# Local attention on one core: masks of head groups side by side, small masking products behind them

## What is computed

```python
Q, K, V = heads(x @ wq), heads(x @ wk), heads(x @ wv)        # 16 heads of 16
i, j = arange(64)[:, None], arange(128)[None, :]
base = (j > i) & (j <= i + 64)                               # window of 64 keys
blk0 = (block > 0) | (j >= 64)                               # block 0 has no block before it
sc = where(base & blk0, einsum(Qb, [K_prev, K_own]) / 4, -inf)
local = softmax(sc) @ [V_prev, V_own]
rem = softmax(where(n <= s // 16, GQ @ pooled(GK).T / 4, -inf)) @ pooled(GV) @ r_out_w
out = (sigmoid(Q . gl) * local + sigmoid(Q . gr) * rem) @ w_out
```

## Time and profile before

| | us |
|---|---|
| median of 3 runs | 2291.6 |
| lowest and highest | 2290.39, 2296.07 |
| the profiled execution | 2287.45 |
| its span, first to last instruction | 2285.7 |
| TensorE busy with products | 2010.9 (88%) |
| VectorE busy | 1642.6 (72%) |
| ScalarE busy | 1221.4 (53%) |

### The profile page before, as it was taken

One profiled execution on the slowest core, in us unless ns is written; L12 is line 12 of the kernel. 1 busy time (PEld: TensorE's weight loads), 2 busy tenths in 40 slices (PEclk: granted clock), 3 DMA queues, 4 the chain that ended last, 5 costly groups with the idle time before them and its releaser, 6 DMA issues. The chain is left out here.

```text
span 2285.7 us, 74481 instructions
## 1 busy us (share of the span) xinstructions
PE 2010.9 (88%) x32248; PEld 1276.1 (56%) x32248; DVE 1642.6 (72%) x2668; ACT 1221.4 (53%) x1870; POOL 495.5 (22%) x804
## 2 busy tenths in 40 slices
PE   3996999999987985798878999999999999999985
PEld 2663565656655654457854555555555555555543
DVE  6776555554546778776676888888888888888847
ACT  3772232313234765223315777777776777777754
POOL 0003000000000000000014544345443544435410
PEclk8998898999999996899967999999999999999997
DMA  3001000000000000342485544545544555455312
GB/s 113 1 1 28 21 2 20 3 20 3 1 21 1 1 1 5 103 144 97 190 294 139 144 128 129 133 127 140 132 128 127 145 142 133 115 138 138 101 29 74
DMA packets 273791, 195.11 MB, mean 85 GB/s; under 512 B 206744, under 2 KB 260310, under 8 KB 273210
## 3 DMA queue, kind: packets, MB, share of 16 engines
q1 hardware_dynamic: 262586, 139.27, 23.9%
q0 software_dynamic: 10496, 50.75, 5.9%
q10 hardware_dynamic: 384, 0.33, 0.0%
HBM read 91.69 MB, written 93.88 MB: 81 GB/s over the span
## 5 line engine op out<-in xcount | busy, mean ns | idle before, releaser
L2158 DVE TENSOR_REDUCE a1c_nm<-a1c_S 128x1 f32<-128x1024 f32 x512 | 609.6, 1218 | 83.6 <-PE a1c_S L2245 83.1
L2092 ACT ACTIVATE a1c_PT<-a1c_ST 128x1024 f32<-128x1024 f32 x499 | 509.8, 1022 | 67.0 <-PE a1c_ST L2245 64.3
L2109 ACT ACTIVATE a1c_Pb<-a1c_S,a1c_nm 128x192 f32<-128x192 f32 (+1 forms) x512 | 212.2, 415 | 202.5 <-DVE a1c_nm L2158 201.2
L2031 POOL TENSOR_TENSOR a1c_lt<-a1c_lt 128x256 f32<-128x256 f32 (+5 forms) x448 | 254.0, 567 | 35.5
L2148 DVE COPY a1c_PbT<-a1c_T 96x512 f32<-96x512 f32 x256 | 175.8, 687 | 98.5 <-PE a1c_T L2277 96.1
L2245 PE MATMUL a1c_ST<-a1c_Q,a1c_KR 57*128 57x256 f16 (+2 forms) x1066 | 176.5, 286 | 29.6 <-ACT a1c_PT L2092 19.3
L2245 PE MATMUL a1c_S<-a1c_KL,a1c_Q 54*32 54x512 f16 (+11 forms) x3136 | 193.7, 327 | 0.3
L2245 PE MATMUL a1c_S<-a1c_KR,a1c_Q 54*32 54x512 f16 (+13 forms) x2816 | 182.0, 317 | 12.8 <-DMA a1c_Gx<-a_bias 10.2
L2245 PE MATMUL a1c_S<-a1c_Gx,ident 64*32 64x96 f32 (+2 forms) x4352 | 186.1, 242 | 0.0
L2023 POOL DMA_DIRECT2D a_band<-a1c_Pb x128 | 71.0, 555 | 494.7 <-ACT a1c_Pb L2109 494.6
L2277 PE MATMUL a1c_T<-ident,a1c_Pb 128*96 128x128 f32 x1024 | 169.5, 289 | 0.8 <-DVE a1c_mhl L2172 0.8
(11 more groups left out here) (366 smaller groups left out, 4096.4 us busy)
## 6 DMA issues: line engine op xcount, KB each, us to landing
a_band<-a1c_Pb POOLq DMA_DIRECT2D x128, 384.0 KB, 3.4
a_bias<-a1b_G SPq DMA_DIRECT2D x32, 768.0 KB, 9.3
a1c_Gx<-a_bias SPq DMA_DIRECT2D x128, 192.0 KB, 4.4
a1c_Dt<-a_band SPq DMA_DIRECT2D x128, 126.0 KB, 3.7
a1c_Q<-a_qk SPq DMA_DIRECT2D x192, 64.0 KB
a1c_Vw<-a_values SPq DMA_DIRECT2D x64, 102.0 KB, 3.0
a1c_KL<-a_qk SPq DMA_DIRECT2D x96, 64.0 KB
a1c_KR<-a_qk SPq DMA_DIRECT2D x90, 64.0 KB
```

The costliest lines, as they stand in the source:

```text
L2031: add = lambda o, x, y: nc.gpsimd.tensor_tensor(o, x, y, ALU.add)
L2092: nc.scalar.activation(PT[:, q % 8, :, :], place(q), ACT.Exp).then_inc(s["exp"], 1)
L2109: nc.scalar.activation(Pb[:, band_slot(I, c), w0:w1], SP[:, t % 2, I * P - 32 + w0:I * P - 32 + w1], ACT.Exp, bias=nm[:, t // 16 % 2, col: ...
L2158: nc.vector.tensor_reduce(nm[:, t // 16 % 2, col:col + 1], SP[:, t % 2, :], AX.X, ALU.max, negate=True).then_inc(s["max"], 1)
```

## The change

In `scores`, the four masks are issued with nothing between them but the two waits (c = 0 and 1, wait, c = 2 and 3), and the four small products follow behind the last mask. In `by_key`, the small products leave the loop over the masks and stand behind all four masks and behind the wait for `mTe`, ahead of the four products with `sel`. The numbers of instructions and their operands are the same. The jobs with g = 1 keep their order.

```diff
-                for c in range(4):
-                    if n == 0 and c % 2 == 0:
-                        pe.wait_ge(s["lmax"], 4 * b + 3 + c // 2)
-                    elif c % 2 == 0:
-                        pe.wait_ge(s["smax"], 2 * (b * NJ + n) - 1 + c // 2)
-                    mm(R[:, c, :], ones64[tri(c), 0:2, :].rearrange("p a x -> p (a x)"), band[tri(c), :, :].rearrange("p a x -> p (a x)"),
-                       start=True, stop=False, skip_group_check=True)
-                    if g == 0:
+                for a in range(2):
+                    if n == 0:
+                        pe.wait_ge(s["lmax"], 4 * b + 3 + a)
+                    else:
+                        pe.wait_ge(s["smax"], 2 * (b * NJ + n) - 1 + a)
+                    for c in (2 * a, 2 * a + 1):
+                        mm(R[:, c, :], ones64[tri(c), 0:2, :].rearrange("p a x -> p (a x)"),
+                           band[tri(c), :, :].rearrange("p a x -> p (a x)"), start=True, stop=False, skip_group_check=True)
+                if g == 0:
+                    for c in range(4):
                         mm(R[0:WIN, c, 0:WIN], ones64[tri(c), 0, :], wall[tri(c), :], start=False, stop=False, skip_group_check=True)
...
                     mm(R[:, c, :], band[tri(c), 0, :], ones64[tri(c), :, :].rearrange("p a x -> p (a x)"), start=True, stop=False,
                        skip_group_check=True)
-                    if job(n - 2)[0] == 0:
-                        mm(R[0:WIN, c, 0:WIN], wall[tri(c), :], ones64[tri(c), 0, :], start=False, stop=False, skip_group_check=True)
...
                     pe.wait_ge(s["mTe"], 2 * b + g + 1)
+                    if g == 0:
+                        for c in range(4):
+                            mm(R[0:WIN, c, 0:WIN], wall[tri(c), :], ones64[tri(c), 0, :], start=False, stop=False,
+                               skip_group_check=True)
```

## The result

The changed kernel takes 2255.97 us (median of 4 runs, 2253.49 to 2260.46) against 2293.75 for the kernel before beside it: a ratio of 0.984, 95% interval 0.982 to 0.986, 37.8 us by the medians and 36.9 by the ratio. A second series gave 2254.53 against 2287.94, ratio 0.985 (0.983 to 0.987), 33 us. The forecast was 2263.6 with a range from 2255 to 2281; the time lies 1 us inside the range's fast end, and the second series' median half a us outside it.

The account below looks back on a forecast made before the run. In the local stage, TensorE's small fixed-cost pieces compete with the trip to VectorE or ScalarE and back. Savings of 3.65 (scores) plus 3.34 (keys) a batch, 28.0 us in four, took 2291.6 to 2263.6 us; range 2255 to 2281.

Parts of the forecast that it names:

- Masks side by side: Changed score and key jobs: four uncovered masks cost 0.54 us, instead of 1.84 with the small products between.
- W: Cost of the four small products behind the masks: taken as 0.20 us, with ends 0.145 and 0.58.
- small products one by one: Rival: small products cost 0.145 us each even side by side; saving 15.8 us, time 2275.8; chance 0.18.
- The trip over VectorE: Score jobs: from one job's products through VectorE's reduction and back to the next job's products, 4.18 us against 4.90 before.
- Key jobs, 4.72: Key jobs 3 to 5: ScalarE's exponentials decide, giving 4.72 us from one masks' block end to the next.
- TensorE waits about 0.9 us in key job 4: Key job 4: TensorE came at 405.43 before and now waits about 0.9 us, as ScalarE sets the pace.
- The cover lost by the first two small products: Small products of c = 0 and 1 now stand behind the second semaphore wait, adding to the trip over the other engine.
- VectorE's remaining cover: Key jobs: VectorE idled 1.60 us before its second reciprocal; job 2 takes 1.10, leaving 0.5.
- The sum, 28.0 us: Local stage: score jobs save 3.65 and key jobs 3.34 us, 6.99 a batch, 28.0 over four batches.
- The same two dips of the clock in each batch: Expected sign: granted clock still falls to 1.2 GHz after the gates and between scores and keys in every batch.
- the dip behind the gates goes away: Rival: the denser block keeps 2.4 GHz after the gates, about 1 to 1.5 us a batch, 2258 us; chance 0.11.
- Waiting lowers the clock in the changed jobs (slower): Rival: TensorE's new waits in five of eight changed jobs bring 1.2 GHz; 12 us slower, 2303.6; chance 0.04.

Follow-up runs that it names:

- the one-half kernel: Changed kernel with all four small products reading operands from the first half of the partitions: 2262.67 us, ratio 0.9885 to the kernel before.
- the kernel by pairs: Changed kernel with two masks, their small products, the wait, then the other two masks and theirs: 2266.78 us, ratio 0.990 to the kernel before.
- the halves: Kernel before with only the score part of the change, 2269.13 us (ratio 0.991), or only the key part, 2275.21 us (ratio 0.994).

## Why the prediction was right

- **Masks side by side, 0.54 us for four.** 0.53 measured. The rows of the jobs with g = 1 were the right ones to price it with.
- **W = 0.20.** 0.18 measured, between the ends 0.145 and 0.58. Halfway between "the second pair is free" and "it costs as much" was near; the one-half kernel shows that even without pairing W would have been 0.24. The high end, and with it the rival of small products one by one (given a chance of 0.18), is refuted: the price was the switch of shapes. So is its variant in which the second pair waits for the first (W up to 0.29): even four products from one half start 0.24 / 4 = 0.06 us apart on average.
- **The trip over VectorE, 4.18 us.** 4.16 measured. **Job 2, ended by TensorE itself, 4.24 us:** 4.21, where it was 5.35. **Key jobs, 4.72:** 4.70.
- **TensorE waits about 0.9 us in key job 4.** The idle time there is 0.52 us: the 0.9 is the distance from the first masks to the third, 393.44 - 392.52 = 0.92, and holds the first two masks too.
- **The cover lost by the first two small products.** Counted whole in W; the kernel by pairs shows the cover was worth 0.03 to 0.04 us a job.
- **VectorE's remaining cover, 0.5 us.** 0.47 measured.
- **The sum, 28.0 us.** 28.4 at full clock, in two profiles of each kernel, and 15.0 and 13.7 in the halves.
- **"The same two dips of the clock in each batch."** This step failed. The rival that the dip behind the gates goes away came true in part, in one or two of four batches, and in these B could be free of it too. The profiles put 3.1 and 6.2 us of the gain down to the clock. That is the part of the gap between forecast and time that the runs show. I had given it a chance of 0.11 as a case apart, all or nothing; it should have been a term of its own in the sum, since the block right behind the gates was among those that the change makes denser.
- **Waiting lowers the clock in the changed jobs (slower).** Refuted: key jobs 3 to 5 keep 4.70 us with up to 0.52 us of waiting (job 4), in all 8 batches of the two profiles.
- **The range.** Its low end adds up to 2258 - 1.8 - 2 = 2254.2 and was written as 2255. The mechanism of the sum was right; that the time stayed inside the written range was partly luck, since nothing in the sum held the clock's part, and the second series' 2254.53 lies between the two figures.

The medians differ by 33 and 38 us; order and clock explain 31 to 35 of it in the profiles. The stages outside the local one took 1783.4 and 1780.9 us in the two profiles before and 1782.7 and 1786.0 in those after, and 1781 to 1791 over all thirteen profiles. So the remainder is inside what differs from run to run. The clock's part, 3 to 6 us, is smaller than that spread too: it rests on the rows of the local stage, and the medians alone could not show it.

## What to carry to other kernels

Put small products of one shape together, and apart from large ones of another: every switch cost about 0.1 us here, and it kept products of different partition halves from running side by side. Price such an edit job by job, asking each time whether TensorE or the trip over the other engine ends last; then look at the granted clock behind the stretch with the thinnest products (here the gates), because a change there can move the clock's cost by as much as several jobs save. Where TensorE has to wait and the clock falls there, useless products in the wait can be worth it: here 18 a batch gained 7 to 9 us.

## What the runs showed of the hardware

The clock's stretches were the surprise. The kernel before showed them the same in two profiles, batch by batch to 0.04 us, 18.0 us in all; the changed kernel had 14.9 and 11.8 us of them, in different batches. The same code with waits of 1.32 and 1.39 us ran once at 2.4 GHz and once at 1.2, and filling the waits held 2.4 GHz in 8 of 8 batches. What decides in the unfilled case is open. The order seems to be part of it (16 of 16 against 19 of 32 dips in A), and what happened earlier in the batch goes with it (no B at full clock behind a dip in A, in 35 batches without fillers), but neither fixes it.
